# Attention scores from two-part float32r splits in 64-row tiles, two heads stacked in the partitions

## What is computed

```python
def _L1_attn_ref(x, w_Q, w_K, w_V):            # 16 heads of 8
    q, k, v = (heads(x @ w) for w in (w_Q, w_K, w_V))
    probs = softmax(einsum('bhtd,bhsd->bhts', q, k) / sqrt(8))
    return merge(einsum('bhts,bhsd->bhtd', probs, v))

def _L1_ffn_ref(inputs, ...):                  # six nodes, each with 8 heads of 16
    for c in range(6):
        q = ew[c, 0] * (nodes[in_q] @ We[eq] + be[eq])      # k and v alike, from other nodes
        o = _mha(q, k, v, Wq[c], Wk[c], Wv[c], Wo[c])
        nodes[c] = act_w[c] * o + q
    return _layernorm(nodes[5], ln_g, ln_b)
```

## Time and profile before

| | us |
|---|---|
| median of 3 runs | 2441.53 |
| lowest and highest | 2424.41 and 2462.66 |
| the profiled execution | 2431.01 |
| its span, first to last instruction | 2429.1 |
| PE busy | 2206.1 |
| DVE busy | 1805.9 |
| ACT busy | 1461.0 |

### The profile page before, as it was taken

One profiled execution on the slowest core, in us unless ns is written; L12 is line 12 of the kernel. 1 busy time (PEld: TensorE's weight loads), 2 busy tenths in 40 slices (PEclk: granted clock), 3 DMA queues, 4 the chain that ended last, 5 costly groups with the idle time before them and its releaser, 6 DMA issues.

```text
span 2429.1 us, 41467 instructions
## 1 busy us (share of the span) xinstructions
PE 2206.1 (91%) x11820; PEld 798.7 (33%) x11820; DVE 1805.9 (74%) x3757; ACT 1461.0 (60%) x2004; POOL 498.1 (21%) x595
## 2 busy tenths in 40 slices
PE   5748868999999999999999999999999999999995
PEld 2224432333233333333333333333333333333331
DVE  6747866778668877777777777777777777778884
ACT  4725541666556666666666666666666666666664
POOL 1101121111111122222222222222222221223433
PEclk9968875999879999999999999999999999999998
DMA  3010124444334466666666666565656566666631
GB/s 94 18 55 32 38 58 70 62 71 72 71 49 74 84 100 98 99 100 99 98 98 98 98 93 90 89 96 94 96 94 96 94 94 98 98 99 103 96 43 32
DMA packets 186460, 196.80 MB, mean 81 GB/s; under 512 B 26424, under 2 KB 149968, under 8 KB 186320
## 3 DMA queue, kind: packets, MB, share of 16 engines
q1 hardware_dynamic: 179792, 193.63, 48.0%
q10 hardware_dynamic: 6528, 1.57, 0.5%
HBM read 75.45 MB, written 23.73 MB: 41 GB/s over the span
## 4 chain that ended last, share of the span: by engine, by line
PE 70%; issue 10%; DVE 10%; ACT 6%; ACTq 2%; DMA 1%; SPq 1%; POOL 1%; DVEq 0%; POOLq 0%
PE bank_o L1023 21%; PE bank_s L985 16%; PE bank_x L1006 14%; PE bank_m L1037 3%; DVE big L1427 3%; PE bank_m L955 2%; PE bank_m L1057 2%; PE bank_m L945 2%; PE bank_m L963 2%; DVE big L1236 2%; PE bank_s L905 1%; ACTq L751 1%; PE bank_m L973 1%; ACT at L712 1%; ACT big L767 1%
## 5 line engine op out<-in xcount | busy, mean ns | idle before, releaser
L1427 DVE TENSOR_REDUCE big<-bank_s 128x1 f32<-128x512 f32 x2048 | 1375.4, 688 | 442.5 <-PE bank_s L985 420.2
L791 ACT ACTIVATE big<-bank_x 128x1024 f32<-128x1024 f32 x1024 | 1048.4, 1025 | 624.5 <-PE bank_x L1006 542.2
L985 PE MATMUL bank_s<-big 96*128 96x512 bf16 (+1 forms) x2048 | 804.2, 393 | 41.0 <-DVE big L1427 27.9
L1006 PE MATMUL bank_x<-big 99*128 99x512 bf16 (+1 forms) x2048 | 623.4, 386 | 2.1 <-ACT big L791 2.1
L1023 PE MATMUL bank_o<-big,at 128*32 128x512 f32 (+1 forms) x5104 | 583.1, 530 | 2.4 <-ACT big L791 2.4
L985 PEld LDWEIGHTS bank_s<-big 96*128 96x128 bf16 (+1 forms) x2048 | 199.9, 98 | 648.3 <-DVE big L1427 472.2
L573 POOL CAST at<-at 128x512 bf16<-128x512 f32 x112 | 68.4, 611 | 1276.3 <-ACT at L721 1022.6
L1006 PEld LDWEIGHTS bank_x<-big 99*128 99x128 bf16 (+1 forms) x2048 | 203.3, 100 | 204.3 <-issue 50.0
L1023 PEld LDWEIGHTS bank_o<-big,at 128*32 128x32 f32 x5104 | 101.6, 109 | 232.5 <-issue 218.8
L580 POOL TENSOR_TENSOR at<-at 128x512 bf16<-128x512 f32 x112 | 129.7, 1158 | 10.1
L575 POOL TENSOR_TENSOR at<-at 128x512 f32<-128x512 f32 x112 | 129.5, 1157 | 8.9
(11 more groups left out here) (149 smaller groups left out, 1635.7 us busy)
## 6 DMA issues: line engine op xcount, KB each, us to landing
big<-at SPq DMA_DIRECT2D x576, 128.0 KB
at<-nodes_d SPq DMA_DIRECT2D x144, 256.0 KB, 8.0
big<-at SPq DMA_DIRECT2D x288, 64.0 KB
nodes_d<-big SPq DMA_DIRECT2D x48, 256.0 KB, 4.3
at<-w_d SPq DMA_DIRECT2D x48, 193.0 KB, 7.9
at<-x2T_d SPq DMA_DIRECT2D x32, 256.0 KB, 7.8
big<-in_x SPq DMA_DIRECT2D x16, 256.0 KB, 2.9
x_d<-big SPq DMA_DIRECT2D x16, 256.0 KB, 6.6
```

The lines of the kernel that those rows point to most:

```text
L791: act.activation(PT[:, kp, h, :, :], bank_x[:, i % 2, :].rearrange("p (c n) -> p c n", c=2), ACT.Exp, scale=x.c.scale).then_inc(S["c_ex"], 1)
L985: pe.matmul(bank_s[:, n % 2, :], qst[0:x.c.R, x.r, h, t * P:(t + 1) * P], kst[0:x.c.R, x.r, h, :], start=True, stop=True).then_inc(S["c_s_ ...
L1006: mm = pe.matmul(sec(bank_x[:, i % 2, :], j), kst[0:x.c.R3, x.r, h, kc_ * P:(kc_ + 1) * P], qst[0:x.c.R3, x.r, h, :], start=True, stop=True)
L1427: dve.tensor_reduce(nm[:, k, n:n + 1], bank_s[:, n % 2, :], AX.X, ALU.max, negate=True).then_inc(S["c_red"], 1)
```

## The change

Queries and keys are split into two parts of type float32r for three of bf16. The contraction has 3 x 16 = 48 rows in node units and 4 x 8 = 32 in attention units, and two more with the maxima (`RM`) for the transposed scores. The 128 partitions hold two heads, head pairs in two halves of 64 (`HALF`); `head_of` and `tile_of` choose the heads so that at a step the transposed scores take the half i % 2 and the row scores the other. `stack` issues two DMAs per term, one per half: 12 per node unit as before, 16 for 18 in attention units, of the same bytes in node units. POOL's split has two instructions for four, DVE's split of the maxima two for four. The maxima are turned by a float32 transpose of 32 columns, and ACT issues two DMAs for one. The order of PE's, DVE's and ACT's work by steps stays, but for the maxima's parts, which DVE now does at step 6 alone. The columns of the weights are permuted on the host to fit. `big` is laid first in memory so that `qst` and `kst` lie over it as float32r.

```diff
-TERMS_16 = [(0, 0), (0, 1), (0, 2), (1, 0), (1, 1), (2, 0)]
-TERMS_8 = [(a, b) for a in range(3) for b in range(3)]
+TERMS_16 = [(0, 0), (0, 1), (1, 0)]
+TERMS_8 = [(a, b) for a in range(2) for b in range(2)]
+HALF = P // 2
+PAIRS = HU // 2
...
+        qst = nc.alloc_sbuf_tensor_at("qst", [P, RING, PAIRS, L], F32R, offset=arena)
+        kst = nc.alloc_sbuf_tensor_at("kst", [P, RING, PAIRS, L], F32R, offset=arena + RING * PAIRS * L * 4)
...
-        mr = cut2(16)
-        mp = cut2(24).bitcast(BF16)
-        mT = cut2(64).bitcast(BF16)
+        mp = cut2(32)
+        mp_r = mp.bitcast(F32R).rearrange("p (f s n) -> p f s n", f=2, s=2)
+        mT = cut2(P).bitcast(F32R)
...
+        def head_of(k, j):
+
+            return GH * k // 2 + j // 2, j % 2
+
+        def tile_of(n):
+
+            return n // 2 % GH ^ 1, 2 * (n // 8) + n % 2
...
+                def rows(to, of, i, part):
+                    for f in range(2):
+                        first = f * HALF + i * x.c.hd
+                        sp.dma_start(to[first:first + x.c.hd, x.r, :, :].bitcast(F32),
+                                     of[f * n // 2:(f + 1) * n // 2, part, :].bitcast(F32)).then_inc(done, 16)
+
                 for i, (_, part) in enumerate(x.c.terms):
-                    sp.dma_start(kst[i * x.c.hd:(i + 1) * x.c.hd, x.r, :, :], k_parts[0:n, part, :]).then_inc(done, 16)
+                    rows(kst, k_parts, i, part)
                 when((S["c_sp"], 2 * x.u + 2))
                 for i, (part, _) in enumerate(x.c.terms):
-                    sp.dma_start(qst[i * x.c.hd:(i + 1) * x.c.hd, x.r, :, :], q_parts[0:n, part, :]).then_inc(done, 16)
+                    rows(qst, q_parts, i, part)
...
                 pool.tensor_copy(dst[:, 0, :], src).then_inc(S["c_pool"], 1)
                 need(pool, S["c_pool"], base + 1)
-                pool.tensor_tensor(src, src, dst[:, 0, :], ALU.subtract).then_inc(S["c_pool"], 1)
-                need(pool, S["c_pool"], base + 2)
-                pool.sem_inc(passed, 1)
-                pool.tensor_copy(dst[:, 1, :], src).then_inc(S["c_pool"], 1)
-                need(pool, S["c_pool"], base + 3)
-                pool.tensor_tensor(dst[:, 2, :], src, dst[:, 1, :], ALU.subtract).then_inc(done, n)
+                pool.tensor_tensor(dst[:, 1, :], src, dst[:, 0, :], ALU.subtract).then_inc(done, n)
...
-                act.activation(mT[0:48, :], bank_m[0:48, 0:P], ACT.Copy).then_inc(S["c_mT_ev"], 1)
+                act.activation(mT[0:32, :], bank_m[0:32, 0:P], ACT.Copy).then_inc(S["c_mT_ev"], 1)
                 need(act, S["c_mT_ev"], G + 1)
-                act.dma_start(qst[x.c.R:x.c.R3, x.r, GH * k:GH * k + GH, :], mT[0:48, :]).then_inc(S["c_m_dma"], 16)
+                for f in range(2):
+                    act.dma_start(qst[f * HALF + x.c.R:f * HALF + x.c.RM, x.r, GH // 2 * k:GH // 2 * (k + 1), :].bitcast(F32),
+                                  mT[16 * f:16 * (f + 1), :].bitcast(F32)).then_inc(S["c_m_dma"], 16)
...
-                h, t = GH * k + n // NT, n % NT
-                pe.matmul(bank_s[:, n % 2, :], qst[0:x.c.R, x.r, h, t * P:(t + 1) * P], kst[0:x.c.R, x.r, h, :],
+                j, t = tile_of(n)
+                h, f = head_of(k, j)
+                rows = slice(f * HALF, f * HALF + x.c.R)
+                pe.matmul(bank_s[:, n % 2, :], qst[rows, x.r, h, t * P:(t + 1) * P], kst[rows, x.r, h, :],
                           start=True, stop=True).then_inc(S["c_s_ps"], 1)
...
-                pe.matmul(bank_m[0:48, 0:P], mp[:, 0:48], identb[:, :], start=True, stop=True).then_inc(S["c_mT_ps"], 1)
+                pe.transpose(bank_m[0:32, 0:P], mp[:, 0:32], ident[:, :]).then_inc(S["c_mT_ps"], 1)
...
-                kp, h = i // GH, GH * k + i % GH
+                kp = i // GH
+                h, f = head_of(k, i % GH)
+                rows = slice(f * HALF, f * HALF + x.c.RM)
...
-                    mm = pe.matmul(sec(bank_x[:, i % 2, :], j), kst[0:x.c.R3, x.r, h, kc_ * P:(kc_ + 1) * P],
-                                   qst[0:x.c.R3, x.r, h, :], start=True, stop=True)
+                    mm = pe.matmul(sec(bank_x[:, i % 2, :], j), kst[rows, x.r, h, kc_ * P:(kc_ + 1) * P],
+                                   qst[rows, x.r, h, :], start=True, stop=True)
...
-                    dve.tensor_copy(mp[:, 0:16], nm[:, k, :]).then_inc(S["c_link"], 1)
-                else:
-                    need(dve, S["c_link"], 3 * G + step)
+                    dve.tensor_copy(mp_r[:, :, 0, :], of).then_inc(S["c_link"], 1)
                 if step == 1:
-                    dve.tensor_tensor(mr, nm[:, k, :], mp[:, 0:16], ALU.subtract).then_inc(S["c_link"], 1)
-                if step == 2:
-                    dve.tensor_copy(mp[:, 16:32], mr).then_inc(S["c_link"], 1)
-                if step == 3:
-                    dve.tensor_tensor(mp[:, 32:48], mr, mp[:, 16:32], ALU.subtract).then_inc(S["c_nm_ok"], 1)
+                    need(dve, S["c_link"], G + 1)
+                    dve.tensor_tensor(mp_r[:, :, 1, :], of, mp_r[:, :, 0, :], ALU.subtract).then_inc(S["c_nm_ok"], 1)
```

More of the change, by code:

```diff
@@ L6 @@
 F32 = mybir.dt.float32
-BF16 = mybir.dt.bfloat16
+F32R = mybir.dt.float32r
 ACT = mybir.ActivationFunctionType
@@ L70, in build @@
         bank_m = ctx.enter_context(nc.psum_tensor("bank_m", [P, 512], F32))
+        arena = -(-nc.sbuf_base // 32) * 32
+        big = sb("big", [P, 30 * 1024])
+        qst = nc.alloc_sbuf_tensor_at("qst", [P, RING, PAIRS, L], F32R, offset=arena)
+        kst = nc.alloc_sbuf_tensor_at("kst", [P, RING, PAIRS, L], F32R, offset=arena + RING * PAIRS * L * 4)
         ident = sb("ident", [P, P])
-        identb = sb("identb", [P, P], BF16)
         half = sb("half", [P, NT])
@@ L120, in build @@
         qf, kf = cut(L), cut(L)
-        qp = cut(3 * L // 2).bitcast(BF16).rearrange("p (t n) -> p t n", t=3)
-        kp_ = cut(3 * L // 2).bitcast(BF16).rearrange("p (t n) -> p t n", t=3)
+        qp = cut(2 * L).bitcast(F32R).rearrange("p (t n) -> p t n", t=2)
+        kp_ = cut(2 * L).bitcast(F32R).rearrange("p (t n) -> p t n", t=2)
         ot_sb = cut(L)
@@ L251, in build @@
             c.R = len(c.terms) * c.hd
-            c.R3 = c.R + 3
+            c.RM = c.R + 2
             c.np_ = HU * c.hd
@@ L298, in stacked @@
         def stacked(x):
-            n = 16 * 2 * len(x.c.terms) * (x.turn + 1)
-            return n + 16 * 2 * len(kc.terms) * QC if x.c.node else n
+            n = 16 * 4 * len(x.c.terms) * (x.turn + 1)
+            return n + 16 * 4 * len(kc.terms) * QC if x.c.node else n
         def loaded(x, n_node, n_first=1):
@@ L554, in _ @@
                 pool.memset(vaug[j], 1.0).then_inc(s_c, 1)
-            pool.wait_ge(s_id, 2)
-            for m in (ident, identb):
-                pool.affine_select(out=m[:, :], in_=m[:, :], compare_op=ALU.not_equal, fill=1.0, base=0,
-                                   pattern=[[-1, P]], channel_multiplier=1).then_inc(s_id, 1)
+            pool.wait_ge(s_id, 1)
+            pool.affine_select(out=ident[:, :], in_=ident[:, :], compare_op=ALU.not_equal, fill=1.0, base=0,
+                               pattern=[[-1, P]], channel_multiplier=1).then_inc(s_id, 1)
             pool.wait_ge(s_c, 7 + NE)
@@ L585, in split @@
                     return
-                base = 3 * UC + 6 * x.un if x.c.node else 3 * x.u
+                base = UC + 2 * x.un if x.c.node else x.u
                 before_ = at_(x.c, x.q, x.r - 1)
@@ L595, in split @@
                     pool.sem_inc(passed, 1)
-                    in_parts(qf, qp, base + 3, S["c_sp"], 1)
+                    in_parts(qf, qp, base + 1, S["c_sp"], 1)
             def residual_rstd(x):
@@ L872, in _ @@
         def _(pe):
-            pe.wait_ge(s_id, 4)
+            pe.wait_ge(s_id, 2)
             pe.wait_ge(s_w, 16 * N_W)
@@ L1426, in reduce @@
                 need(dve, S["c_s_ps"], 16 * (2 * x.u + k) + n + 1)
-                dve.tensor_reduce(nm[:, k, n:n + 1], bank_s[:, n % 2, :], AX.X, ALU.max, negate=True).then_inc(S["c_red"], 1)
+                j, t = tile_of(n)
+                at_n = j % 2 * 8 + j // 2 * NT + t
+                dve.tensor_reduce(nm[:, k, at_n:at_n + 1], bank_s[:, n % 2, :], AX.X, ALU.max, negate=True).then_inc(S["c_red"], 1)
             def parts(x, k, step):
@@ L1433, in parts @@
                 G = 2 * x.u + k
+                of = nm[:, k, :].rearrange("p (f n) -> p f n", f=2)
                 if step == 0:
@@ L1518, in _ @@
                 reduce(at_(kc, 0, 0), 0, n)
-            for step in range(4):
+            for step in range(2):
                 parts(at_(kc, 0, 0), 0, step)
@@ L1535, in body @@
                             reduce(*group)
-                            if i in (6, 7):
-                                parts(*read_group(c, q, r, k), 2 * (i - 6) + j)
+                            if i == 6:
+                                parts(*read_group(c, q, r, k), j)
                         if (k, i) == (0, paced(x, 5, 7)):
```

(2 more changed lines are left out.)

12 lines of the change are left out of this document (3 added, 9 removed).

## The result

The changed kernel takes 2983.2 us (median of four runs, 2968.9 to 2990.5), the kernel before 2452.1 us in the same measurement (four runs, 2424.4 to 2502.1): a ratio of 1.225, 95% interval 1.215 to 1.236. It is slower by over a fifth. The forecast was 2410 us, in a range of 2330 to 2550 us.

A forecast was written before the change was run, and what follows sets the result against it. TensorE was taken as the bound, with ScalarE's queue setting one stretch per half unit. Node units -24 us, attention units 0 and start -3 us took 2431.0 to 2404 us; the forecast was put at 2410 us, range 2330 to 2550 us.

The forecast's parts named there:

- The failed step: The 16 attention units: gains and costs balance at 0, from -8 to +13 us.
- The clock as a rival: TensorE, idler at the ring's turns after 1000 us, loses its clock at three more: +60 us, 2470 us; chance 0.03.
- a clock below 1.00 between 1000 and 2200 us: Granted clock in that stretch: falling below 1.00 would show the prediction wrong; no size or chance of its own.
- The slower rivals: Score matmuls of a step: no overlap or two float32r passes, 2545 us, chance 0.20; both together, 3000 us, chance 0.05.
- the halves don't overlap: Score matmuls run one after another, about 1.05 us for four: 2545 us; chance 0.20, shared with two passes.
- two passes: Float32r score matmuls take two passes side by side, about 1.05 us for four: 2545 us; chance 0.20, shared with no overlap.
- both failing: No overlap and two passes together: a step grows to 1.9 us, some 10 us per unit, 3000 us; chance 0.05.
- The score matmuls: Four score matmuls of a node step: 0.74 us for 0.97, a gain of 0.23; bounds 0.61 to 1.05 us.
- How many steps keep it: Nine of a node unit's 16 steps keep the 0.23 us gain, 2.1 us; ScalarE, VectorE or the projection set the others.
- Tiling changes: Switches between 64-row scores and full-array projections in a node unit: cost 0.3 us, from 0 to 1.3 us.
- The maxima: Second DMA issue on ScalarE, 0.63 us twice per unit: cost 1.3 us before the turning, from 0.6 to 1.8 us.
- The node unit: Whole node unit: -2.1 + 0.3 + 1.3 = -0.5 us, to 30.7 us; over 48 units -24 us.

The follow-up runs named there:

- the run with one DMA: Changed kernel with ScalarE issuing only one of the maxima's two DMAs and the exponential's scale set to 0: 2907.2 us, measured once.
- the two best versions: Changed kernel, all units 62 and 64 rows, maxima's DMAs issued by GpSimd: 2351.5 us; kernel before, attention units 96 and 99 rows, same issue: 2371.5 us.

## Why the prediction was wrong, point by point

**The failed step: the attention units, priced at nothing.** The prediction put their balance at 0, from -8 to +13 us. They cost 495 us, so it is this term of the sum that failed. It saw that "rows of 32 and 34 may even be different tilings" with nothing side by side, which came true, but priced it at 0.08 us for each change at full clock. At full clock the lost overlap would have been some 42 us and the changes perhaps 74 us; most of the rest is the half clock. It never asked what the fewer rows, down from 72 to 32, would do to the clock, though the earlier trace rows showed the clock low in just these units: 0.88 and 1.00 in the two stretches shown, with 72 and 75 rows, where the node units, with 96 and 99, had 1.00. That row was read as the cost of stalls at the ring's turns.

**The clock as a rival.** It stood there with 0.03 and +60 us, placed at the turns of the node units, argued from idleness before the clock falls. In the changed kernel it stays at 0.50 while TensorE is never idle. What was wrong is the mechanism: idleness may start the low clock, as in the kernel before, but here few rows at work kept it low, and more rows alone, of zeros, brought it back. The prediction did name a clock below 1.00 between 1000 and 2200 us as a sign against itself, and it came: 0.50 from 1000 to 1200 us, where the attention units now stand, and 0.96 to 0.97 in the node units. The Trainium skill, "TensorE: Matmul & The Clock Gate", Part 1, says that the clock follows how busy the array has recently been. With busy time as the trace counts it, this case disagrees: 200 of 200 us at 0.50.

**The slower rivals.** One pass and overlap both hold where rows exceed 32, so neither "the halves don't overlap" nor "two passes" is what happened in the node units. That both failing was put at 3000 us, near the measured 2983, is chance: that sum has 10 us more in each of 48 node units, and the loss lies in the 16 others.

**The score matmuls.** Predicted 0.74 us for four, measured 0.66; both halves start within 0.01 us. It holds. The two pairs take 0.34 and 0.32 us (1813.98, 1814.32, 1814.64), some 0.1 us more than they stream: that is in the place of the load of 0.11 us, whose record is 0.18 us, and the 0.08 us for the change of tiling don't come on top. The upper bound, 1.05 us without overlap, measured 1.14 with 62 and 64 rows on the same half.

**How many steps keep it.** Nine were counted. Step by step between 1821.99 and 1852.26 us, against 1584.62 to 1615.64 us before, five are shorter, by 0.26 to 0.31 us, and the others hardly change or are longer. After the exchange, steps that were TensorE's alone meet VectorE's reduces: at 1823.65 us a second row score starts 0.54 us after the first, for 0.33 without that wait. Five times 0.3 us is -1.5 us per unit in place of -2.1.

**Tiling changes.** Taken at 0.3 us per unit, with 1.3 us as the bound. A step with a projection (1802.10 to 1804.15, 2.05 us) is longer than such a step before (about 1.97) although its four scores are shorter: it waits 0.29 us for L757, and from the start of the projection to the next score it is 1.03 us for 0.94. With -1.5 us, twice 0.54 us for the issues and a unit 0.2 us shorter than before, the rest is 0.2 us, near the value taken (nothing, if an issue is worth the 0.7 us of the run with one DMA). The Trainium skill, "TensorEngine Tiling (Array Packing)", Key Properties, says that a change of mode drains TensorE; the 0.1 us by which the next score starts later would fit that, but the longer weight load would show in the same place, and no run here tells them apart.

**The maxima.** The two issues take 1.27 us, 0.63 us each as predicted for the second; against the one of 0.73 us that is 0.54 us more. The turning waits 1.17 us (1.3 predicted), and leaving the second out gives 0.7 us per half unit, 67 us over 48 units. That is as predicted in place and size.

**The node unit.** Away from the ring's turns it takes 30.8 us (turnings at 1821.40 and 1852.26), where 30.7 were predicted, but the kernel before takes 31.0 there (1584.62 and 1615.64): the prediction's 31.2 was a mean with the turns in it, so 0.2 us were won and not 0.5. A turn of the ring has become dearer, 21.2 us between two turnings (1768.33 and 1789.48) for a half unit of 15.4:

```profile
1782.36 0.70 PE L997 MATMUL bank_s<-kst,qst 48*128 48x512 f32 x1 [2.60 <-DVE big L1443]
```

TensorE idles 2.60 us, and the granted clock from 1780 to 1790 us is 0.62. Eight turns, from 1656 to 2575 us, take 4 to 6 us more than a half unit, where they took 1.1 to 1.3 us more before: about half of the 70 us behind the attention units. The rest is half units of 16.6 to 18.0 us, behind a turn, in the last units, and scattered between, in some of which the clock is low for a short while (0.83 from 1748 to 1758 us). The clock rival had put 20 us on each of three turns, 60 us in all: near that sum in size, but a small part of the whole.

**What stays open.** The runs show that the rows at work and the overlap make the difference, but not by which rule the chip judges: 62 and 64 rows on the same half held 1.00 from 450 to 600 us, and 0.67 from 700 to 900. Several of the runs were made once. Whether few columns would do the same was not tried, nor whether the data in the added rows matters (zeros in the queries against ones in the keys). Why the clock after a ring's turn takes longer to come back in the changed node units, and how much of the 30 us between the two best versions is the halves', is not settled.

## What to carry to other kernels

Before cutting the rows that a matmul contracts, look at the granted clock of the stretch: fewer rows can cost the clock, and with it up to twice the time of everything on TensorE, although the instructions stay the same. Where small contractions are wanted, place them in opposite halves with more than 32 rows on both sides so that they run side by side, and fill up the rows with zeros, which costs no column. And move DMA issues off an engine whose queue a critical wait stands behind: here four issues of some 0.6 us per unit, moved to GpSimd, gave 80 us.

## What the runs showed of the hardware

- A granted clock of 0.50 held from 392 to 1290 us with TensorE busy for 897.9 of 898 us, in units of 32 and 34 rows; it was 0.98 with 62 beside 64 rows and the same columns.
- Rows of zeros count: padding 72 and 75 rows to 96 and 99 made the kernel before 1.7% faster (interval 1.1 to 2.2%).
- The clock was at 0.50 after waits of 1 to 3 us (1.04, 1.45 and 2.80 us in three places), while most of the waits of 1.17 us in the changed node units didn't lead to it; how soon it came back differed with the rows.
- 32 and 34 rows in opposite halves do not run side by side, 33 and 35 do, and start within 0.01 us.
- A float32r matmul of 512 columns takes 0.235 us at full clock behind another, about as bf16 (0.22 us); its weight load of 128 columns shows as 0.18 us, a bf16 one as 0.10 us.
- Two DMA issues one after another on ScalarE took 1.27 us, one of them alone 0.63 us, the single one of the kernel before 0.73 us.
